# Interleaved head pairs in q and k, direct copies of the first two batches' rows, and products of a zero tile in two places

## What is computed

```python
q = (side + b_self) @ Wq + bq
k = concat([x + b_prev, side + b_self], 1) @ Wk + bk
v = concat([x, side], 1) @ Wv + bv
score_prev = q · k[:, :, :256] * SCALE            # 256 x 256 per head, masked by seq_len
score_self = (q * k[:, :, 256:]).sum(-1) * SCALE  # one per query
w = softmax(concat([score_prev, score_self]))
x = x + (w_prev @ v_prev + w_self * v_self) @ Wo + bo
# then: a = tanh(x @ W1 + b1) @ v1; masked softmax p over the tokens (mask by kind);
x = x + (p @ x) / count
```

## Time and profile before

| | |
|---|---|
| Time, median of 3 runs | 281.02 us (279.83 to 283.24) |
| Profiled execution, its own time | 281.62 us |
| Its span, first to last instruction | 279.9 us |
| Mean granted TensorE clock over the span | 0.950 |
| PE busy | 238.4 us (85%) |
| DVE busy | 184.4 us (66%) |
| ACT busy | 156.6 us (56%) |
| POOL busy | 76.3 us (27%) |
| DMA | 35.5 MB, mean 127 GB/s |

### The profile page before, as it was taken

One profiled execution on the slowest core, in us unless ns is written; L12 is line 12 of the kernel. 1 busy time (PEld: TensorE's weight loads), 2 busy tenths in 40 slices (PEclk: granted clock), 3 DMA queues, 4 the chain that ended last, 5 costly groups with the idle time before them and its releaser, 6 DMA issues.

```text
span 279.9 us, 6089 instructions
## 1 busy us (share of the span) xinstructions
PE 238.4 (85%) x2100; PEld 187.4 (67%) x2100; DVE 184.4 (66%) x384; ACT 156.6 (56%) x297; POOL 76.3 (27%) x87
## 2 busy tenths in 40 slices
PE   2986898599979999999999989999999769886732
PEld 2984787367758777877788768777787455563622
DVE  2659655457469758875887588758985885335631
ACT  4351223376477557755785667557856546772430
POOL 8026011013025103610451035103511330316111
PEclk9999669599999999999999999999999997999977
DMA  5469636913865096609560946096409410011011
GB/s 152 103 235 233 138 112 182 210 31 115 242 142 188 5 248 134 228 16 252 119 227 20 256 108 225 18 246 118 150 33 261 95 72 2 8 34 37 0 40 37
DMA packets 28021, 35.50 MB, mean 127 GB/s; under 512 B 4440, under 2 KB 24416, under 8 KB 28000
## 3 DMA queue, kind: packets, MB, share of 16 engines
q1 hardware_dynamic: 27360, 33.12, 44.6%
q0 software_dynamic: 640, 2.10, 2.0%
HBM read 20.26 MB, written 14.69 MB: 125 GB/s over the span
## 4 chain that ended last, share of the span: by engine, by line
PE 59%; DVE 13%; DMA 9%; issue 8%; ACT 5%; SPq 3%; POOL 1%; ACTq 0%; DVEq 0%; POOLq 0%
PE ps_any L1080 20%; PE ps_any L1134 10%; PE ps_max L1108 9%; PE ps_any L1087 6%; DMA k_rows<-k_spill 5%; PE ps_exp L1121 4%; DVE s_max L887 4%; DMA k_spill<-k_lo 3%; PE ps_any L1184 3%; PE ps_any L1240 2%; DVE bv_cast L854 2%; SPq L418 1%; ACT pt L623 1%; PE ps_any L1200 1%; PE ps_any L1166 1%
## 5 line engine op out<-in xcount | busy, mean ns | idle before, releaser
L887 DVE TENSOR_REDUCE s_max<-ps_max 128x4 f32<-128x1024 f32 x64 | 78.1, 1220 | 25.1 <-PE ps_max L1108 25.1
L623 ACT ACTIVATE pt<-ps_exp 128x1024 f32<-128x1024 f32 x64 | 65.6, 1025 | 50.1 <-PE ps_exp L1121 49.5
L1108 PE MATMUL ps_max<-k_rows,q_rows 49*128 49x256 f32 x256 | 33.7, 343 | 13.0 <-DMA k_rows<-k_spill 7.2
L1108 PEld LDWEIGHTS ps_max<-k_rows,q_rows 49*128 49x128 f32 x256 | 20.2, 194 | 24.6 <-DVE s_max L887 10.4
L1134 PE MATMUL ps_any<-pt,v_aug 128*32 128x256 f32 x512 | 36.0, 401 | 0.0
L1121 PE MATMUL ps_exp<-q_rows,k_rows 51*128 51x256 f32 x256 | 27.0, 288 | 2.3 <-ACT pt L623 2.3
L578 POOL TENSOR_TENSOR attn<-num,rden 128x256 f32<-128x256 f32 x16 | 9.6, 621 | 54.0 <-DVE rden L1030 54.0
L1121 PEld LDWEIGHTS ps_exp<-q_rows,k_rows 51*128 51x128 f32 x256 | 20.3, 191 | 4.1 <-ACT pt L623 2.7
L569 POOL TENSOR_TENSOR prod_lo<-prod,prod_hi 128x512 fp32r<-128x512 f32 x8 | 10.3, 1282 | 42.2 <-ACT prod_hi L714 42.2
L1080 PE MATMUL ps_any<-st_hi,w_hi 128*128 128x256 f32 x64 | 20.9, 326 | 0.3 <-DVE st_lo L912 0.3
L1134 PEld LDWEIGHTS ps_any<-pt,v_aug 128*32 128x32 f32 x512 | 13.7, 112 | 10.5 <-issue 1.3
(11 more groups left out here) (145 smaller groups left out, 605.3 us busy)
## 6 DMA issues: line engine op xcount, KB each, us to landing
q_rows<-q_spill SPq DMA_DIRECT2D x32, 192.0 KB, 4.4
k_rows<-k_spill SPq DMA_DIRECT2D x32, 192.0 KB
q_spill<-q_hi SPq DMA_DIRECT2D x16, 256.0 KB, 2.5
k_spill<-k_hi SPq DMA_DIRECT2D x16, 256.0 KB, 2.5
s_sb<-in_fside_BxSxS SPq DMA_DIRECT2D x8, 256.0 KB, 3.7
x_sb<-in_x SPq DMA_DIRECT2D x8, 256.0 KB, 3.2
q_spill<-q_lo SPq DMA_DIRECT2D x8, 256.0 KB, 2.2
k_spill<-k_lo SPq DMA_DIRECT2D x8, 256.0 KB, 3.1
```

Source lines behind the costliest of these rows:

```text
L623: nc.scalar.activation(pt[:, 2 * j % 8:2 * j % 8 + 2], ps_exp[:], ACT.Exp).then_inc(p_ready, 1)
L887: nc.vector.tensor_reduce(s_max[:, j // MJ, :, :, j % MJ].rearrange("p t e -> p e t"), ps_max[:], AX.X, ALU.max).then_inc(max_found, 1)
L1108: last = pe.matmul(ps_max[:, e, t], q_rows[par][rows, j, P * t:P * t + P], k_rows[par][rows, j, :], start=True, stop=True)
```

## The change

1. Feature order. A half of q or k now holds the features of every other pair, so partition p of a half is (e, d, g, l): head of the pair, feature, group, pair within. The weights' split (L640, L798), the biases' loads (four DMAs in place of two), `headsum` (two reductions in place of one), `self_scores` and the copy `s_self` follow this order. The spill tensors are [3, 128, 2, 256], so a spill writes 2 KB of a partition in one piece. The placement still reads 4 KB pieces.
2. Direct copies. For batches 0 and 1 no spill and no placement: `direct` copies each part from SBUF to the rows, six DMAs of 128 KB for q and six for k, each from 64 partitions into 16, and a mask DMA. Batch 0's four k_hi copies are issued from ScalarE, all others from SP. SP issues batch 1's input loads behind batch 0's copies.
3. Because the copies write over the ones, `ones_rows(1)` moves to the end of GpSimd's setup, ahead of its period -1.
4. VectorE: in period -1 `k_low` stands ahead of `product`. `bias_out` moves from the end of period -1 to period 0, step 2. ScalarE: `weight_hi(3)` moves from behind `k_hi` to behind `prod_hi`.
5. Zero tile. VectorE zeroes `idle` (128 x 256) first. TensorE multiplies it, 128 x 128 by 128 x 256 columns, result not read: 13 times ahead of everything (behind `idle_set`), and at the end of a step: 10 in period -1 step 1 (behind TX, ahead of Q), 10 in period 8 step 4 (behind AT, ahead of WO), 16 in period 8 step 13 (behind SB, ahead of PT), 10 in period 9 step 0 (behind PT, ahead of PO).

```diff
+IDLE = {(-1, -1): 13, (-1, 1): 10, (8, 4): 10, (8, 13): 16, (9, 0): 10}
...
+        def direct(queue, part, rows, sixteens, sent):
+            for c in sixteens:
+                for e in range(2):
+                    queue.dma_start(rows[64 * e + DH * c:64 * e + DH * c + DH].bitcast(F32),
+                                    part[P // 2 * e:P // 2 * e + P // 2].rearrange("p m t -> p (m t)").bitcast(F32)
+                                    ).then_inc(sent, 16)
...
-                            sp.dma_start(dram[:, c].rearrange("e p t -> p e t"), parts[part][:].bitcast(F32)
-                                         ).then_inc(spilled, 16)
+                            sp.dma_start(dram[c], parts[part][:].bitcast(F32)).then_inc(spilled, 16)
...
+            def direct_q(i, k):
+                if i * 2 + k == 0:
+                    sp.wait_ge(rows_one, 2)
+                sp.wait_ge(q_copied, count(i, k, 1, 1))
+                direct(sp, q_hi, q_rows[k % 2], (0, 1), q_direct)
+                sp.wait_ge(q_lo_done, count(i, k, 1, 1))
+                direct(sp, q_lo, q_rows[k % 2], (2,), q_direct)
+
+            def direct_k(i, k):
+                if i * 2 + k > 0:
+                    sp.wait_ge(k_hi_done, count(i, k, 1, 1))
+                    direct(sp, k_hi, k_rows[k % 2], (0, 2), k_direct)
+                else:
+                    sp.wait_ge(masks_stored, 16)
+                mask = row(mask_dram, i, k).unsqueeze(0).unsqueeze(0).broadcast_to([2, NJ, S])
+                sp.dma_start(k_rows[k % 2][R_MASK:R_MASK + 65:64].bitcast(F32), mask).then_inc(k_direct, 16)
+                sp.wait_ge(k_lo_done, count(i, k, 1, 1))
+                direct(sp, k_lo, k_rows[k % 2], (1,), k_direct)
...
+                if isinstance(i, int) and 2 * i + k < 1:
+                    direct_q(*nxt)
+                    if live(*b):
+                        place_max(*b, 0)
+                    direct_k(*nxt)
+                    if not live(*b):
+                        load(i, k + 2)
+                    if live(*prv) and not last:
+                        load_again(*prv)
+                    return
...
+            ones_rows(1)
             def split_lo(...)
...
-                if first:
-                    ones_rows(1)
...
                         if first:
-                            weight_hi(3)
+                            act.wait_ge(rows_one, 2)
+                            act.wait_ge(k_hi_done, 1)
+                            direct(act, k_hi, k_rows[0], (0, 2), k_direct)
...
+                        if first:
+                            k_low(*c)
+                            product(*c)
+                        else:
+                            product(*c)
+                            k_low(*c)
...
+            nc.vector.memset(idle[:].bitcast(F32), 0.0).then_inc(idle_set, 1)
             weight_lo(0)
...
+            def idle_behind(i, k, s):
+                if isinstance(i, int):
+                    out_of = ps_exp[:, 1, 1] if i < 0 else ps_max[:, 1, 1]
+                    for _ in range(IDLE.get((2 * i + k, s), 0)):
+                        pe.matmul(out_of, idle[:, 0:P], idle[:], start=True, stop=True)
```

More of the change, by code:

```diff
@@ L372, in build, with parts_free @@
         out_rows = out.rearrange("b (t p) d -> b p t d", p=P)
+        def direct(queue, part, rows, sixteens, sent):
[4 more added lines that the diff above has]
+                                    ).then_inc(sent, 16)
+        def parts_free(engine, i, k, spilled, direct_sent, sent_per):
+            if isinstance(i, int) and 0 < 2 * i + k < 3:
+                engine.wait_ge(direct_sent, sent_per * (2 * i + k))
+            elif (n := count(i, k, 48, -96)) is not None:
+                engine.wait_ge(spilled, n)
         block = ctx.enter_context(nc.Block())
@@ L392, in spill @@
                 n_parts = held(count(i, k, 1, 1))
-                if (n := held(count(i, k, placed_per, 0))) is not None:
+                if (n := held(count(i, k, placed_per, -2 * placed_per))) is not None:
                     for half in placed:
@@ L447, in period @@
                     mask = row(mask_dram, *nxt).unsqueeze(0).unsqueeze(0).broadcast_to([2, MJ, S])
-                    n_spilled = held(count(*nxt, 48, 48))
+                    n_spilled = held(count(*nxt, 48, -48))
                     n_scored = [held(count(*nxt, NJ, MJ * (g + 1) - 2 * NJ)) for g in range(NM)]
@@ L535, in split_lo @@
                 pool.wait_ge(hi_done, count(i, k, 1, 1))
[L536 to L537 removed]
+                parts_free(pool, i, k, spilled, q_direct, 96)
                 nc.gpsimd.tensor_tensor(lo[:], full[:], hi[:].bitcast(F32), ALU.subtract).then_inc(lo_done, 1)
@@ L694, in period @@
                         act.wait_ge(k_ready, count(*c, 1, 1))
-                        if (n := count(*c, 48, 0)) is not None:
-                            act.wait_ge(k_spilled, n)
+                        parts_free(act, *c, k_spilled, k_direct, 112)
                         for m in range(2):
@@ L769, in q_copy @@
                 last.then_inc(q_full_done, 1)
-                if (n := count(i, k, 48, 0)) is not None:
-                    act.wait_ge(q_spilled, n)
+                parts_free(act, i, k, q_spilled, q_direct, 96)
                 for m in range(2):
@@ L904, in group_max, with product, k_low @@
                                                op0=ALU.mult, op1=ALU.subtract).then_inc(neg_done, 1)
+            def product(i, k):
+                dve.wait_ge(ks_ready, count(i, k, 1, 1))
+                dve.wait_ge(q_full_done, count(i, k, 1, 1))
+                if (n := count(i, k, 1, 0)) is not None:
+                    dve.wait_ge(prod_lo_done, n)
+                    dve.wait_ge(prod_hi_done, n)
+                for m in range(2):
+                    last = nc.vector.scalar_tensor_tensor(
+                        out=prod[:, m], in0=ps_any[:, bank_of("KS", i, k), m],
+                        scalar=bqk_col[:, 2, m:m + 1], in1=q_full[:, m], op0=ALU.add, op1=ALU.mult)
+                last.then_inc(prod_done, 1)
+            def k_low(i, k):
+                dve.wait_ge(k_hi_done, count(i, k, 1, 1))
+                parts_free(dve, i, k, k_spilled, k_direct, 112)
+                for m in range(2):
+                    last = nc.vector.scalar_tensor_tensor(
+                        out=k_lo[:, m], in0=ps_any[:, bank_of("K", i, k), m],
+                        scalar=bqk_col[:, 1, m:m + 1], in1=k_hi[:, m].bitcast(F32),
+                        op0=ALU.add, op1=ALU.subtract)
+                last.then_inc(k_lo_done, 1)
             def period(i, k):
@@ L977, in period @@
                     for c in at("prod", i, k, s):
-                        dve.wait_ge(ks_ready, count(*c, 1, 1))
-                        dve.wait_ge(q_full_done, count(*c, 1, 1))
-                        if (n := count(*c, 1, 0)) is not None:
-                            dve.wait_ge(prod_lo_done, n)
-                            dve.wait_ge(prod_hi_done, n)
-                        for m in range(2):
-                            last = nc.vector.scalar_tensor_tensor(
-                                out=prod[:, m], in0=ps_any[:, bank_of("KS", *c), m],
-                                scalar=bqk_col[:, 2, m:m + 1], in1=q_full[:, m], op0=ALU.add, op1=ALU.mult)
-                        last.then_inc(prod_done, 1)
-                        dve.wait_ge(k_hi_done, count(*c, 1, 1))
-                        if (n := count(*c, 48, 0)) is not None:
-                            dve.wait_ge(k_spilled, n)
-                        for m in range(2):
-                            last = nc.vector.scalar_tensor_tensor(
-                                out=k_lo[:, m], in0=ps_any[:, bank_of("K", *c), m],
-                                scalar=bqk_col[:, 1, m:m + 1], in1=k_hi[:, m].bitcast(F32),
-                                op0=ALU.add, op1=ALU.subtract)
-                        last.then_inc(k_lo_done, 1)
+                        if first:
+                            k_low(*c)
[3 more added lines that the diff above has]
+                            k_low(*c)
                     for c in at("masked", i, k, s):
@@ L1160, in self_scores @@
             def self_scores(bank):
-                by_block = bank[:, 0, 0:2 * H].rearrange("p (g t e j) -> p t e g j", g=NM, t=KB, e=2)
+                by_block = bank[:, 0, 0:2 * H].rearrange("p (g t m x) -> p t m g x", g=NM, t=KB, m=2)
                 for t in range(KB):
-                    for e in range(2):
+                    for m in range(2):
                         for part in (prod_hi, prod_lo):
-                            last = pe.matmul(by_block[:, t, e], part[:, e, P * t:P * t + P], headsum[:],
+                            last = pe.matmul(by_block[:, t, m], part[:, m, P * t:P * t + P], headsum[:],
                                              start=(part is prod_hi), stop=(part is prod_lo))
```

61 lines of the change are left out of this document (37 added, 24 removed).

## The result

The changed kernel takes 362.25 us (median of four runs, 361.76 to 365.33), the kernel before, run beside it on the same chip, 282.13 us (279.83 to 285.58). The ratio is 1.290, 95% interval 1.277 to 1.303. I had predicted 273.3 us. Some executions of a kernel are a per cent or more longer at a lower granted clock; the ratios in this document leave them out and the medians do not, so the two can differ by some tenths of a per cent. The profiled execution took 361.76 us, its span is 360.1 us: 80.2 us more than the 279.9 of before.

The account below looks back on a forecast made before the run. It took TensorE to bound the middle periods, leaving gains only at both ends. Terms 0.9 + 3.8 + 1.3 + 0.2 + 1.5 = 7.7 us brought 281.6 to 273.9, hence 273.3 us at the median; range 267 to 278.5.

Parts of the forecast that it names:

- Batches 2 to 7: Batches that still spill: placement pieces unchanged, only spill pieces grow to 2 KB; gain 0.2 us, bounds 0 and 1.
- Landing time of a direct copy: Copies for batches 0 and 1: taken as 3.0 us from issue to landing, since a spill takes 3.27.
- rival D: Batches 0 and 1: direct copies land late, gain used up from about 8 us; about 285 us at 10; chance 0.04.
- the part on the Trainium skill: Period 0: 104 GB/s into partitions 0 to 15, so four k_hi copies take about 2.5 us, 0.3 us later.
- The start: Up to batch 0's first reduction: cast held until 10.8, score tile 0 at 27.8; gain 0.9 us, bounds -0.8 and 4.4.
- Period 0 and 1: Direct copies shorten waits, clock partly rises: gain 3.8 us in period 0, 1.3 at the beginning of period 1.
- the 1.2 us for the clock: Period 0: part of its gain, 1.2 of the 4.1 us that full clock would save in the low stretch.
- The end: Zero products hold the fast clock through PT and PO: gain 1.5 us, bounds -1.6 and 1.6.
- Rival C: Prologue and end: zero products do nothing for the clock; gain 5.9 us, 275.1 us; chance 0.10.
- A: Rival: the clock holds from the prologue on, no low stretch in period 0; gain 12.8 us, 268.2 us; chance 0.20.
- B: Rival: held cast and clock together, start -0.8, low clock through period 0; gain 3.8 us, 277.2 us; chance 0.24.

Follow-up runs that it names:

- experiment 2: Kernel before with 8 rows of padding behind each third of the spill tensor, so a placement's outermost count is 3: 384.37 us, ratio 1.381.
- experiment 9: Changed kernel with the 48 rows of a half of q and k ordered by column (3d + c instead of 16c + d): 278.03 us, ratio 0.999.
- experiment 10: As experiment 9, and GpSimd's second fill of ones waits for the cast of the bias inputs: 275.86 us, ratio 0.988.
- experiment 12: As experiment 10, without the 23 zero products of the prologue: 273.67 us, ratio 0.984.
- experiment 5: Changed kernel with the old layout of q and k and no zero products, direct copies kept, from 128 partitions of 1 KB: 288.46 us, ratio 1.035.
- experiment 7: Kernel before with GpSimd's second fill of ones moved early, behind its setup: 284.03 us, ratio 1.016.
- experiment 11: Kernel before with the interleaved layout alone, rows by column, no direct copies or zero products: 278.93 us, ratio 0.999.
- experiment 3: Kernel before with all 59 zero products: 281.35 us, ratio 1.008.
- experiment 4: Kernel before with the 36 zero products of the end alone: 278.21 us, ratio 0.991.
- experiment 8: Kernel before with 36 zero products at the end, `k_low` ahead of `product`, `bias_out` in period 0, fills behind the cast: 279.40 us, ratio 0.998.
- experiment 1: Changed kernel with the spill tensor ordered so a placement has 48 rows outermost, each spill as two DMAs: 307.26 us, before 281.01.
- experiment 6: Kernel before with five groups of twelve 128 KB copies behind its last scores: groups took 14.7, 10.8, 9.8, 13.9 and 15.3 us.

## Why the prediction was wrong

**The step that failed** is the term "Batches 2 to 7": "The placement's pieces are 4 KB as before; only the spill's grow from 1 to 2 KB", gain 0.2. I compared the size of the pieces, which is indeed the same, and didn't look at the order of the counts in the access pattern, though the diff shows `(c d)` turned into `c d`. That one sentence stands for +66.1 us between batches 2 and 7 and most of the +7.1 in period 1. None of the four rivals contained it. The middle periods, which I gave nothing because TensorE bounds them, came to wait for the placements, once a period:

```profile
172.72 0.80 PE L1178 MATMUL ps_max<-k_rows,q_rows 49*128 49x256 f32 x4 [6.90 <-DMA k_rows<-k_spill]
```

These 6.90 us are less than half of what the period from 129.89 on lost (42.83 us instead of 27.83). TensorE is idle for 4.5 us more at four other places (2.07, 1.21, 0.98 and 0.26), one of them behind the late load of `xr_sb`, and the same work keeps it busy for 31.41 us instead of 27.01, at a granted clock of 0.86 instead of 1.00: the clock fell during the wait (0.71 from 122.94 to 129.89) and was 0.50 in the row from 129.89 to 133 above.

Experiments 2 and 9 show this from both sides, adding the fault to the old kernel (+13.5 us a period) and taking it out of the new one (27.78).

**Landing time of a direct copy: mis-sized.** I took 3.0 us from the spill's row, and forecast that it would be "not late". The last k_lo copy of batch 0 was issued from 22.8 to 23.4 (forecast 22.4) and TensorE went on at 33.22: 10 us. In batch 1 it took 5.3:

```profile
51.88 5.34 DMA k_rows<-k_lo
```

This is rival D, which I gave 0.04, with "about 8 us" as the landing time that uses up the gain. Its mechanism and its place were right. What stood against it, 1.6 MB at 240 GB/s, was a rate read from transfers into 48 partitions; into 16 neighbouring ones it is 118, and 1.57 MB then take 13.3 us. In the part on the Trainium skill I put its 104 GB/s to four copies, as if those to other ports ran beside them, and made 0.3 us of it; applied to all twelve in a row it gives 15 us, as an estimate, and the warning was there.

**The start otherwise was right.** The timeline has the held cast and its releaser's end:

```profile
8.17 2.56 DVE L859 CAST bin_parts<-bin_col 128x4 fp32r<-128x4 f32 x1 [0.80 <-DMA bqk_raw<-in_L_cond_bk]
...
8.90 1.80 POOL L561 MEMSET k_rows<- 128x2048 f32 x1
...
12.10 0.27 PE L1231 MATMUL ps_max<-bin_parts,w_hi 128*128 128x4 f32 x1 [0.87 <-DVE w_lo L848]
```

The cast is held to 10.73 (forecast 10.8), the bias products start at 12.10 (12.4), TensorE is ready for score tile 0 at 33.22 - 6.30 = 26.9 (27.8). The Trainium skill's rule on the shared port (SBUF — State Buffer, Who interferes with whom) holds for 4 elements as for 128. The repair of experiments 10 and 12 is the wait that undoes it.

**Period 0 and 1.** In the changed kernel nothing of their terms can be read, since 4.06 us of waiting and the placements cover them. Experiment 9 is the change as I had imagined it. By its profile the terms are -0.8 at the start (forecast 0.9), 1.4 in period 0 (3.8), 0.7 in period 1 (1.3), 0.2 in batches 2 to 7 (0.2) and 1.3 at the end (1.5), in all 2.8 of 7.7. So even without the fault the forecast was too good, and the ratio of 0.999 says that what is left is within the noise. (The terms go by score tile 0; by its reduction, as I had forecast, the start is -0.4.) The landing is again mis-sized, about 6 us instead of 3.0 (issued at 22.7, used at 29.0), but costs only the 0.66 us of the wait. TensorE itself was ready at 28.35 and not at 26.67 as before, since from 24.71 on its products start 0.21 us apart and `bv_product` takes 1.72 us instead of 1.13:

```profile
26.64 1.72 PE L1251 MATMUL ps_exp<-w_raw,bv_cast 128*128 128x256 f32 x4
```

I had kept the fast clock there; period 0 has a granted clock of 0.78, hardly better than the 0.75 of before, so the 1.2 us for the clock were not earned. In experiment 12 the cast is free: 0.9, 4.2, 2.2, -0.7 and 2.7, in all 9.4, in an execution that is the fastest of its six.

**The end was right in its mechanism.** PT takes 0.63 us and the products of PO start 0.12 us apart, with the 16 and 10 zero products between:

```profile
348.55 2.26 PE L1221 MATMUL ps_max<-idle 128*128 128x256 f32 x16
351.38 0.63 PE L1153 MATMUL ps_any<-ident,pool_p 128*128 128x128 f32 x4 [0.56 <-ACT pool_p L804]
351.76 1.43 PE L1221 MATMUL ps_max<-idle 128*128 128x256 f32 x10
...
353.78 0.29 PE L1260 MATMUL ps_any<-x_hi,pool_pt_lo 128*128 128x256 f32 x1
353.90 0.28 PE L1260 MATMUL ps_any<-x_hi,pool_pt_hi 128*128 128x256 f32 x1
```

Its size is less certain. Behind batch 7's first tile the changed kernel takes 64.3 us, 2.0 more than before, with a clock of 0.79 and 0.72 in the first two stretches of 10 us. In the profiles of kernels whose middle is not slow it is 62.3 to 63.5 us without these zero products (before, 5, 7, 11) and 59.6 to 61.0 with them (3, 4, 9, 12), but 64.7 and 62.2 in experiments 8 and 10, whose profiled executions were among the longest of their kernels. That experiment 9's 1.3 comes so close to 1.5 is partly luck.

Rival C, zero products do nothing for the clock, falls with PT and PO. Rivals A and B can't be judged in the changed kernel. In experiment 9 A falls, with a clock of 0.78 in period 0 and 2.8 of its 12.8 us. B's products at the lower level up to `bv_product` are there, and its sum of 3.8 is nearer than the forecast's 7.7; but in both kernels K and KS ran mostly at the lower level, where B had them at the fast one.

**Open.** Whether experiment 8's edits gain anything that the clock's differences between executions then hide; whether the prologue's zero products cost what separates 10 from 12; and how experiment 1's 31 us divide between the doubled spills and the waits behind them.

## What to carry to other kernels

When a diff alters the view of a DRAM tensor in a DMA, write down the counts of both sides from the outermost in and see whether two of them still merge: same bytes and same piece size say nothing about how many engines carry them. A low DMA share beside a wait for a DMA is the sign in a profile. Look at the destination's partitions too, how many they are and how far apart, and take a rate only from rows with the same: here the order of the rows in SBUF, free for the arithmetic, decided both.

## What the runs showed of the hardware

- A placement of 192 KB with outermost counts 3 and 48 ran at an engines' share of 0.21 to 0.26 in the stretch with its neighbours, against 0.91; the period grew from 27.8 to 41 us (experiment 2 and the changed kernel).
- Twelve copies into 16 neighbouring partitions ran at 118 to 126 GB/s, from SBUF and from DRAM, with the engines at a share of 0.95 to 1.15; into every third partition of 48 at 145 to 201, at 1.02 to 1.11. A full share thus says that engines hold packets, not that they move at their rate.
- A cast of 4 elements was held for 2.56 and 3.00 us beside two fills of 1.80 us, and did not get in between them.
- That the prologue's zero products raise the clock early is only in part shown. The products' distance falls from 0.21 to 0.12 us at 9.9 us in the changed kernel, at 10.5 and 11.0 in experiments 10 and 9, and is 0.12 from 8.1 on in experiment 3; all have these zero products. Of the kernels without them the kernel before and experiments 2, 4 and 7 get there only at 20.1 to 22.2, but 5, 6, 8, 11 and 12 at 10.1 to 12.1. Experiment 6 has the same code up to there as the kernel before, and gets there at 10.41:

```profile
10.18 0.21 PE L1191 MATMUL ps_max<-bin_parts,w_hi 128*128 128x4 f32 x1
10.24 0.31 PE L1191 MATMUL ps_max<-bin_parts,w_lo 128*128 128x4 f32 x1
10.41 0.25 PE L1191 MATMUL ps_max<-bin_parts,w_hi 128*128 128x4 f32 x1
10.52 0.25 PE L1191 MATMUL ps_max<-bin_parts,w_lo 128*128 128x4 f32 x1
```

- In the changed kernel it was lost again at once. The clock is 1.00 from 9.8 to 13.2 us, with PE busy 2.53 of 3.40 us, and then at the lower level through a stretch in which PE had no gap:

```profile
9.80:13.20 3.40, 2.53 (x22) 2.33 (x21) 3.21 (x9) 0.73 (x2) 0.90 (x1) 1.00 0.44 128
13.20:20.00 6.80, 6.80 (x32) 6.53 (x31) 4.33 (x18) 2.41 (x6) 1.28 (x1) 0.50 0.19 48
```
